# Second layer's loop written out: second products four units behind, four hid buffers, three decay buffers, two scans at the end of each turn

## What is computed

```python
xn = _layernorm(x, axis=-1)
x = x + _L1_attn_ref(xn, ...) + _L1_ffn_ref(xn, ...)

# _L1_attn_ref: 4 sequences of 512 tokens, H = 128 features, N = 16 states each
dt = jax.nn.softplus(jnp.einsum('bth,gh->btg', u, W_dt) + b_dt)
def step(state, inp):
    dt_t, u_t = inp
    dtA = dt_t[..., None]
    A_bar = jnp.exp(dtA * A)
    state = A_bar * state + dtA * B_mat * u_t[..., None]
    y_t = jnp.einsum('bhn,hn->bh', state, C_mat) + D_vec * u_t
    return (state, y_t)

# _L1_ffn_ref, 64 experts of 32 hidden columns, the best 8 per token
def body(acc, p):
    W1, B1, W2, B2, e = p
    h = jax.nn.silu(xf @ W1 + B1) @ W2 + B2
    cw = jnp.sum(jnp.where(ti == e, tw, 0.0), axis=-1)
    return (acc + cw[:, None] * h, None)
```

## Time and profile before

| | us |
|---|---|
| median of 3 runs (545.20 to 549.20) | 545.24 |
| the profiled execution | 539.09 |
| its span, first to last instruction | 537.3 |
| PE busy in the span | 449.7 |
| DVE busy | 384.4 |
| ACT busy | 277.9 |
| POOL busy | 184.1 |

### The profile page before, as it was taken

One profiled execution on the slowest core, in us unless ns is written; L12 is line 12 of the kernel. 1 busy time (PEld: TensorE's weight loads), 2 busy tenths in 40 slices (PEclk: granted clock), 3 DMA queues, 4 the chain that ended last, 5 costly groups with the idle time before them and its releaser, 6 DMA issues.

```text
span 537.3 us, 7545 instructions
## 1 busy us (share of the span) xinstructions
PE 449.7 (84%) x2143; PEld 329.6 (61%) x2143; DVE 384.4 (72%) x702; ACT 277.9 (52%) x392; POOL 184.1 (34%) x187
## 2 busy tenths in 40 slices
PE   2739999999999999999999693996887797797782
PEld 1327887888788887788777562454553464454442
DVE  6687488845887468864698978682786696596684
ACT  2375655336643474514644368437647746755720
POOL 1148015301133013320012004600765854865650
PEclk9959999999999999999999798598989988998996
DMA  6320001100002000000000000000575676666664
GB/s 176 90 67 15 2 0 42 43 0 0 27 13 51 0 0 0 0 0 1 0 2 0 1 1 0 2 0 0 105 146 102 124 135 116 123 126 118 127 118 117
DMA packets 29532, 26.72 MB, mean 50 GB/s; under 512 B 10837, under 2 KB 25414, under 8 KB 29510
## 3 DMA queue, kind: packets, MB, share of 16 engines
q0 software_dynamic: 4608, 16.78, 16.4%
q1 hardware_dynamic: 24902, 9.69, 7.2%
HBM read 8.64 MB, written 1.05 MB: 18 GB/s over the span
## 4 chain that ended last, share of the span: by engine, by line
PE 46%; DVE 27%; ACT 11%; issue 10%; POOL 3%; DMA 2%; DVEq 1%; ACTq 0%; SPq 0%; POOLq 0%
PE psum L202 9%; PE psum L1090 8%; PE psum L204 8%; PE psum L203 8%; PE psum L1262 6%; DVE hid L772 2%; PE psum L1210 2%; ACT dec L641 2%; PE psum L1254 2%; POOL state L433 2%; ACT L652 2%; DVE state L978 1%; DVE xn_tok L694 1%; DVE hid L987 1%; PE psum L1225 1%
## 5 line engine op out<-in xcount | busy, mean ns | idle before, releaser
L565 ACT ACTIVATE sil<-psum 128x512 f32<-128x512 f32 (+1 forms) x96 | 56.3, 596 | 104.6 <-PE psum L204 91.2
L772 DVE TENSOR_TENSOR hid<-sil,psum 128x512 f32<-128x512 f32 (+1 forms) x96 | 65.0, 685 | 51.8 <-PE psum L204 32.6
L1090 PEld LDWEIGHTS psum<-e_w,hid 128*128 128x128 f32 (+1 forms) x768 | 94.9, 191 | 6.0
L1090 PE MATMUL psum<-e_w,hid 128*128 128x128 f32 (+1 forms) x768 | 95.3, 274 | 0.0
L202 PE MATMUL psum<-xn_hi,e_hi 128*128 128x512 f32 (+1 forms) x192 | 81.5, 424 | 8.5 <-DVE hid L772 7.9
L987 DVE TENSOR_TENSOR hid<-sil,psum 128x512 f32<-128x512 f32 x64 | 42.6, 673 | 47.0 <-ACT sil L652 43.5
L204 PE MATMUL psum<-xn_lo,e_hi 128*128 128x512 f32 (+1 forms) x192 | 75.7, 395 | 0.0
L978 DVE TENSOR_TENSOR_SCAN state<-dec,win_t 128x1024 f32<-128x1024 f32 x32 | 75.7, 2366 | 0.0
L203 PE MATMUL psum<-xn_hi,e_lo 128*128 128x512 f32 (+1 forms) x192 | 75.6, 394 | 0.0
L652 ACT ACTIVATE sil<-psum,vec_t 128x512 f32<-128x512 f32 x64 | 43.1, 687 | 60.0 <-PE psum L204 33.8
L202 PE MATMUL psum<-xn_hi,g_hi 128*128 128x512 f32 x64 | 51.5, 804 | 26.7 <-ACT sil L652 26.7
(11 more groups left out here) (261 smaller groups left out, 760.7 us busy)
## 6 DMA issues: line engine op xcount, KB each, us to landing
xn_tok<-state POOLq DMA_DIRECT2D x32, 512.0 KB, 4.7
e_raw<-in_L_ffn_w SPq DMA_DIRECT2D x16, 128.0 KB, 2.1
e_raw<-in_L_ffn_w SPq DMA_DIRECT2D x8, 176.0 KB, 2.3
res<-in_L_attn_x SPq DMA_DIRECT2D x4, 256.0 KB, 3.6
g_raw<-in_L_ffn_w SPq DMA_DIRECT2D x16, 64.0 KB, 3.2
g_w<-in_L_ffn_w SPq DMA_DIRECT2D x16, 64.0 KB, 3.8
out<-res SPq DMA_DIRECT2D x4, 256.0 KB, 2.9
e_raw<-in_L_ffn_w SPq DMA_DIRECT2D x16, 48.0 KB, 1.9
```

What stands on the lines that cost most here:

```text
L565: act.activation(sil[0:M, s % 2, :], ps[s % 2][0:M, :], ACT.Silu).then_inc(silu_done, 1)
L772: dve.tensor_tensor(hid[0:M, tb % 2, ft, :], sil[0:M, s % 2, :], ps[2 + s % 2][0:M, :], ALU.mult).then_inc(gated, 1)
L1090: ins = pe.matmul(ps[4 + o % 2][:, n * P:(n + 1) * P], hid[0:m, tb % 2, ft, n * P:(n + 1) * P], e_w2[j][0:m, ft, :], start=(ft == 0), stop ...
```

## The change

The loops of PE and ACT in the second layer are written out: waits are on constants, and the nops that carried counts into the loops (`hid_done`, `scanned`, `h_silu`, `g_out` started at 2 or 4) go. There are four hid buffers, so weigh c waits for second product c - 4. There are three decay buffers, used in turn by state number; a decay waits for the scans three states back, and the first element of each third buffer is cleared by one more memset. On PE, second products come four units behind; at a turn's end stand first and factor products of the next turn's first two units, then the last four second products. On DVE a turn is scan 0, three weighs, scan 1, five weighs, scan 2, scan 3. SP's loop stays, with its count changed. POOL's order stays as it was.

```diff
-        dec = [later(f"dec_{j}", [P, NTOK], dec_at + j * 4 * NTOK) for j in range(2)]
+        DECS = 3
+        dec = [later(f"dec_{j}", [P, NTOK], dec_at + j * 4 * NTOK) for j in range(DECS)]
...
-        hid_ring = [hid[:, r, 0, :] for r in range(2)]
+        HRING = 4
+        hid_ring = [hid[:, r % 2, r // 2, :] for r in range(HRING)]
...
-                    sp.wait_ge(g_out, i * GSTEPS + (j + 1) * NBLK + 2)
+                    sp.wait_ge(g_out, i * GSTEPS + (j + 1) * NBLK)
...
-                    pool.wait_ge(scanned, i * SCANS + k + 1 + SCANS)
+                    pool.wait_ge(scanned, i * SCANS + k + 1)
...
-            def decay(i, j):
-
-                act.wait_ge(scanned, i * SCANS + 2 * j + 2)
-                act.nop().then_inc(act_passed, 1)
...
+            def decay(n):
+
+                if n >= DECS:
+                    act.wait_ge(scanned, 2 * (n - DECS) + 2)
...
+            def silu(c):
+
+                act.wait_ge(h_made, c + 1)
+                if c >= 2:
+                    act.wait_ge(hid_done, c - 1)
...
+            for i in range(NG // GPI):
+                for c in range(i * GSTEPS, (i + 1) * GSTEPS):
+                    silu(c)
+                if i < NG // GPI - 1:
                     for j in range(GPI):
-                        decay(i + 1, j)
...
+                        decay((i + 1) * GPI + j)
...
-                dve.wait_ge(g_out, c + 1)
-                dve.tensor_tensor(hid_ring[s % 2], sil[:, s % 2, :], ps[2 + s % 2][:, :], ALU.mult
+                if c >= HRING:
+                    dve.wait_ge(g_out, c - HRING + 1)
+                dve.tensor_tensor(hid_ring[c % HRING], sil[:, c % 2, :], ps[2 + c % 2][:, :], ALU.mult
...
-            def group_turn(i):
-                weigh(i, 0)
-                for k in range(SCANS):
-                    scan(i, k)
-                    weigh(i, 2 * k + 1)
-                    if k + 1 < SCANS:
-                        weigh(i, 2 * k + 2)
-
             for i in range(NG // GPI):
-                group_turn(i)
...
+                c = i * GSTEPS
+                scan(i, 0)
+                for s in (0, 1, 2):
+                    weigh(c + s)
+                scan(i, 1)
+                for s in (3, 4, 5, 6, 7):
+                    weigh(c + s)
+                scan(i, 2)
+                scan(i, 3)
...
+            for i in range(NG // GPI):
+                c = i * GSTEPS
+                for s in range(2, GSTEPS):
+                    expert_in(c + s)
+                    if s >= 4:
+                        expert_out(c + s - 4)
+                for s in range(2):
+                    if c + GSTEPS + s < UNITS:
+                        expert_in(c + GSTEPS + s)
+                for s in range(GSTEPS - 4, GSTEPS):
+                    expert_out(c + s)
```

More of the change, by code:

```diff
@@ L409, in _ @@
             pool.wait_ge(sp_exp, 1)
-            for j in range(GPI):
+            for j in range(DECS):
                 own(pool.memset(dec[j][:, :].rearrange("p (b t) -> p b t", t=TB)[:, :, 0:1], 0.0))
@@ L658, in _ @@
-            act.nop().then_inc(h_silu, 2)
-            act.wait_ge(win_ready, NBLK)
-            for j in range(GPI):
-                decay(0, j)
-            with act.Fori(0, NG // GPI - 1) as i:
-                group_turn(i, False)
-            group_turn(NG // GPI - 1, True)
+                               scale=ssm_a[:, n:n + 1]).then_inc(decay_ready, 1)
+            def silu(c):
+                act.wait_ge(h_made, c + 1)
+                if c >= 2:
+                    act.wait_ge(hid_done, c - 1)
+                act.activation(sil[:, c % 2, :], ps[c % 2][:, :], ACT.Silu,
+                               bias=vec_t[:, V_B1 + c // NBLK:V_B1 + c // NBLK + 1]).then_inc(h_silu, 1)
@@ L667, in _ @@
+            act.wait_ge(win_ready, NBLK)
+            for n in range(GPI):
+                decay(n)
+            for i in range(NG // GPI):
+                for c in range(i * GSTEPS, (i + 1) * GSTEPS):
+                    silu(c)
+                if i < NG // GPI - 1:
+                    for j in range(GPI):
+                        decay((i + 1) * GPI + j)
         @block.vector
@@ L1277, in _ @@
-            with pe.Fori(0, NG // GPI - 1) as i:
-                group_turn(i, False)
-            group_turn(NG // GPI - 1, True)
+                    pe.wait_ge(g_w2_in[g % GPI], (g // GPI) * 16 + 16)
+                pe.wait_ge(hid_done, c + 1)
+                pe.matmul(ps[4 + tb][:, :], g_w2[g % GPI][:, :], hid_ring[c % HRING], start=False,
+                          stop=g == NG - 1, skip_group_check=True).then_inc(g_out, 1)
+            UNITS = NG * NBLK
+            for c in range(2):
+                expert_in(c)
```

63 lines of the change are left out of this document (20 added, 43 removed).

## The result

The changed kernel takes 575.06 us (median of 4 runs, 573.73 to 576.61), the kernel before took 545.22 beside it (539.66 to 549.20): ratio 1.058, 95% interval 1.050 to 1.067, slower. The profiled executions stand 576.29 to 539.09, spans 574.5 to 537.3, so the traces differ by 37.2 us, more than the medians (29.8). The executions of the kernel before run from 538.36 us at a mean granted clock of 0.936 to 549.82 at 0.905 (the profiled one: 539.09 at 0.938), and a ratio is taken over the fast ones alone while a median is over all, so that a ratio can differ from the quotient of its two medians by up to 0.7%.

The account below looks back on a forecast made before the run. The second layer's expert loop was taken as a cycle of PE, ACT and DVE with ACT's decays as its hole. -0.6 + 6 x (21.8 - 19.4) + 7.8 = +21.6 on 545.2 gave 567 us, range 546 to 586.

Parts of the forecast that it names:

- Second products behind, wider buffers, third decay buffer: Hole at the turn's end: PE's gap before unit 10's first product falls from 3.45 to 1.9 us; alone, some two microseconds less.
- Scan and scale exclude each other: DVE against POOL: the first to start has the way for 0.88 (L433) or 2.2 us (scan); the other waits whole.
- Rival 3: Weights arrive before PE wants them, scales running beside scans: 17.2 us per turn, 531 us; chance 0.08.
- Scale 2 gets in before scan 0: Turn's end: POOL's scale 2 starts at 6.0 behind scan 3, holds scan 0 back 0.9 us, done at 7.1.
- rival 1: DVE keeps the way through all three scans: weights at 16.0, turns of 24.3 us, 584 us; chance 0.2.
- the forecast's chain: POOL at the turn's end: scale 2 done at 7.1, scale 3 at 10.2, the second group's weights at 14.4 us.
- The row that misled: Old trace, two L932 operations on DVE: POOL's L418 got in between, the second taking 1.51 instead of 1.23 us.
- Clock: PE behind its 3.5 us gap: half rate loses 1.7 us, charged in half the turns.
- First turn: Expert loop's first turn, no scan pair before it: 18.8 instead of 19.4 us, so -0.6.
- Six turns: The six turns between first and last: 21.8 us each instead of 19.4.
- Last turn: From the last turn's first silu until DVE goes on after the DMA: 28.5 us instead of 20.7, +7.8.
- Rival 2: POOL slips in before scan 1: weights at 12.6, turns of 19.2 us, 549 us, no change; chance 0.1.

Follow-up runs that it names:

- experiment 1: Changed kernel with the old order on VectorE, buffers and written-out loops kept: 533.53 us against 538.66, ratio 0.988.
- experiment 4: Changed kernel with POOL's four scales of a turn replaced by memsets that only write: 526.78 us against 538.66, ratio 0.974.
- experiment 5: Changed kernel with scan 0 of a turn waiting by semaphore for the end of the turn before's scan 3: 574.65 us against 544.68, ratio 1.060.
- experiments 11 and 12: Changed kernel with POOL's scale 2 cut in two pieces of varied width (574.43 us), then with its arrival and factor varied by turn (575.05 us).
- experiment 7: Changed kernel with 16 further matmuls on TensorE in its wait for the weights, in seven turns: 559.10 us against 538.95, ratio 1.034.
- experiment 12: Changed kernel with POOL's scale 2 delayed by memsets in some turns and given a constant factor in others: 575.05 us in one run, against 544.67.
- experiment 6: Changed kernel with the second group's weights ahead of scales 2 and 3 in POOL's order: 544.17 us against 544.68, ratio 1.002.
- experiment 10: Changed kernel with VectorE's scans spread, only scan 3 and the next scan 0 adjacent, POOL's order kept: 522.57 us, ratio 0.963.

## Why the prediction was right, and where it was off

Right: slower, inside the range, and by the mechanism of the sum (the scans hold the scales, the scales the weights, the weights PE). 567 was forecast, 575 measured; on medians +29.8 where +21.6 stood. By steps:

- *Second products behind, wider buffers, third decay buffer.* PE's gap before in(10) was forecast at 1.9 and is 1.63; ACT's 7.20 stayed (430.73 to 437.93). Taken alone, this was to shorten the turn "by some two microseconds": it was 0.7 (experiment 1, 18.69 against 19.4). There PE waits for VectorE's weighs (16.3 us in all, up to 1.6) and ACT too (26.2 in all).
- *Scan and scale exclude each other.* Right: 5.11 and 3.37, and experiment 4 takes it away. But "the first to start has the way" doesn't hold by the starts that the profile shows: in the earlier trace rows L433 starts 0.07 ahead of the scan and waits, in the earlier trace rows 0.09 ahead and goes first; g_hi in experiment 5 starts 0.17 ahead and waits, scale 3 in the changed kernel 0.20 ahead and goes first. At such distances the outcome can't be read from the starts. Rival 3 needed scans and scales to run side by side; its premise made real gave 17.2 per turn, as it said, and 526.78 us, 11.9 less than the kernel before beside it, where the rival had 14.
- *Scale 2 gets in before scan 0.* This step failed: it starts behind scan 0 and is done at 9.3, not 7.1, which is the first half of rival 1. The forecast and rival 1 both then went wrong on scan 1 in opposite ways. Scale 3 began 0.20 before scan 1 and held it up, where rival 1 had it lose and the weights come at 16.0. They came at 14.8, beside 14.4 forecast: that this time was met is luck, since scale 2 came 2.2 later than forecast and the wait of g_hi for scan 1 fell away. Experiment 5 ran the forecast's chain as written and got the same turn: this failed step cost nothing.
- *The row that misled.* The earlier trace rows showed a POOL operation that got in between two of DVE's. I overlooked two things. `at_q<-at_q` has no second name, while the scale reads `state,ssm_cb`, the difference that experiments 11 and 12 show to matter. And the two L932 are issued through `own`, which makes the second wait for the first by a semaphore (it starts 0.04 us behind the first one's end; a scan starts 0.08 before the end of the scan ahead of it): an opening like that of experiment 5, where the scale got in with its factor. Either would do, and no run tells which it was there. The rival reading (that DVE leaves no opening) came true in all seven turns of the changed kernel, but in 2 of 35 cases it fails.
- *Clock.* This is the term of the sum that was mis-sized. "A clock mean of 0.91 over 19.6 us is 3.5 us at half rate, 1.7 us lost; I charge it in half the turns": 0.85 per turn. It came in every turn (0.78 to 0.93 from the second on, mostly 0.86), and cost 2.3 to 2.6 behind six of the seven waits, 1.6 behind the first (experiment 7). From in(12) to the last silu I had 6.1 + 0.35; it took 8.84 at the lower clock, and 6.36 where PE was kept busy. Clock 1.6 and weights 0.4 too little are the 2.0 between 21.8 and 23.8.
- *First turn* 18.8 forecast, 18.73 measured, in part by luck: it passed at a granted clock of 0.83, which the forecast didn't have in it. In experiment 12, where nothing is changed in that turn, it took 17.74 at 0.90. *Six turns* at 21.8, measured 23.6 on average. *Last turn* 28.5 forecast, 31.5 measured: the last silu is 16.7 behind the first instead of 14.3, which is again the lower clock and the wait, and the landing took 5.3 behind scale 3 instead of 4.9.
- *Rival 2* (POOL slips in before scan 1, then no change) asked for the weights in time. Its outcome, not its race, is experiment 6.

By the traces: -0.6 + 6 x (23.6 - 19.4) + 10.8 = +35.4, and 1.6 ahead of the loop make the 37.2 but for rounding.

## What to carry to other kernels

Before putting operations with two SBUF inputs in a row on VectorE, look at what GpSimd has queued behind the operation that they will hold up, and when it is due: here a wait of 3 us was free in one order, and of 5 cost 5.8% in another, because the weights stood behind it. Moving the urgent work ahead in the blocked engine's queue took the loss back without touching the scans; spreading the scans made the kernel 3.7% faster than before (experiment 10), of which buffers and loops alone gave 1.2% (experiment 1). When a wait falls on TensorE alone and is as long as here (3.7 to 4.4 us), charge the lower clock behind it in every turn, at what the same matmuls take at that level.

## What the hardware showed unexpectedly

A GpSimd operation that waits for VectorE is let in between two VectorE operations that stand in a row or isn't, and its operands go far to tell which: with a factor read per partition from SBUF it waited for all of them in 33 of 35 cases (4.35 to 5.11 us, whatever its length and arrival) and for one in the other 2 (3.00), with a constant for one both times (2.93, and 2.18 for 128 columns). Where VectorE stood at a semaphore between the two, the first kind got in as well (3.00, experiment 5). Only these widths, factors and scans were tried, the constant in two turns of one execution; how it comes about, and what let the two in, stays open. (The Trainium skill, SBUF — State Buffer, section "Who interferes with whom", says that issue order and not the operation's shape decides who is blocked. For length the runs agree; for the factor experiment 12 differs, at 2.93 and 2.18 us, and the measurement decides.)

And 16 matmuls into a bank that is overwritten anyway gained some 2.5 us per turn by what came behind them: at 3.80 us of work in a wait of 4.4, TensorE stayed at 1.00 in all turns from the second on but one (0.92, where the clock fell before the fill).
